# Packing the causal diagonal of a rational-softmax attention into equal pairs, on one NeuronCore

## The reference, cut to what matters

```
h     = x @ W[cat] + b[cat]
q,k,v = h @ w_qkv.T                       # 16 heads of 32
s     = (q . k) / sqrt(32) - slope * |i - j|,  NEG where j > i
num   = 0.5 * (1 + s * rsqrt(1 + s*s))
probs = num / (sum(num) + 1e-6)
x     = x + (probs @ v) @ w_out.T
z     = LayerNorm(x + relu(x @ W1 + b1) @ W2 + b2) * gamma + beta
x     = x + dequant(int8(z / scale) @ w_int8.T) + bias     # scale from max|z| of everything
```

## Time and profile before

| | us |
|---|---|
| Median of 3 runs | 2266.02 (2264.18 to 2266.58) |
| The profiled execution's own time | 2265.64 |
| Its span, first to last instruction | 2263.8 |
| Busy in the span: DVE | 1878.6 (83%) |
| PE | 1803.9 (80%) |
| POOL | 1715.7 (76%) |
| ACT | 1685.0 (74%) |
| Granted TensorE clock, mean | 0.907 of full speed |

### The profile page before, as it was taken

How to read it: one execution, slowest core, us unless ns; L and a number is a source line. 1 busy time by engine, 2 the same in 40 slices (tenths; PEclk the granted TensorE clock), 3 DMA queues, 4 the chain that set the end, 5 groups by cost and what they waited for, 6 DMA issues and landing times.

```text
span 2263.8 us, 31228 instructions
## 1 busy us (share of the span) xinstructions
PE 1803.9 (80%) x10640; PEld 904.5 (40%) x10640; DVE 1878.6 (83%) x2114; ACT 1685.0 (74%) x1938; POOL 1715.7 (76%) x784
## 2 busy tenths in 40 slices
PE   5678877877787789998888877877787787887864
PEld 4555323333333346664444433333333333342331
DVE  4358888888889888889789898888888888899768
ACT  0247897989889888889567667999889888767413
POOL 2136887788878887788678887788878887788548
PEclk9899988988898899999999998988988898998879
DMA  5411111110111022202322221110111021121137
GB/s 176 146 49 44 49 30 35 43 45 25 40 40 49 20 69 66 68 25 74 84 77 81 69 54 34 40 49 21 45 40 48 20 79 44 42 62 52 59 123 237
DMA packets 126620, 138.68 MB, mean 61 GB/s; under 512 B 27868, under 2 KB 78044, under 8 KB 126044
## 3 DMA queue, kind: packets, MB, share of 16 engines
q1 hardware_dynamic: 126460, 136.64, 21.5%
HBM read 54.02 MB, written 22.80 MB: 34 GB/s over the span
## 4 chain that ended last, share of the span: by engine, by line
PE 38%; ACT 21%; DVE 20%; issue 12%; POOL 4%; DMA 2%; SPq 2%; DVEq 0%; POOLq 0%; ACTq 0%
ACT yb L669 9%; PE sc L825 7%; PE ov L804 7%; ACT yb L671 7%; DVE gb L1042 6%; PE dn L804 6%; ACT gb L661 6%; DVE gb L983 5%; PE it L723 5%; PE it L740 4%; PE it L747 4%; PE it L727 3%; POOL oT L654 2%; SPq L428 2%; PE it L707 1%
## 5 line engine op out<-in xcount | busy, mean ns | idle before, releaser
L623 POOL TENSOR_TENSOR yb<-yb 128x1024 f32<-128x1024 f32 (+3 forms) x640 | 1510.2, 2373 | 460.9 <-DVE gb L1042 448.6
L669 ACT ACTIVATE yb<-sc 128x1024 f32<-128x1024 f32 (+3 forms) x640 | 566.9, 886 | 376.3 <-PE sc L825 189.8
L1042 DVE TENSOR_TENSOR gb<-sc,yb 128x1024 f32<-128x1024 f32 (+3 forms) x640 | 676.6, 1057 | 186.1 <-ACT yb L671 183.9
L983 DVE TENSOR_TENSOR gb<-gb,yb 128x1024 f32<-128x1024 f32 (+3 forms) x640 | 779.2, 1218 | 3.9 <-ACT gb L661 0.5
L825 PE MATMUL sc<-qmv,kst 128*128 128x512 f32 (+3 forms) x1280 | 505.6, 472 | 295.8 <-DVE gb L1042 278.2
L671 ACT ACTIVATE yb<-yb 128x1024 f32<-128x1024 f32 (+3 forms) x640 | 595.0, 930 | 20.3
L661 ACT ACTIVATE gb<-gb 128x1024 f32<-128x1024 f32 (+3 forms) x640 | 584.1, 913 | 0.1
L825 PEld LDWEIGHTS sc<-qmv,kst 128*128 128x128 f32 x1280 | 238.7, 209 | 648.3 <-DVE gb L1042 453.3
L804 PE MATMUL ov<-gb,vv 128*32 128x512 f32 (+3 forms) x2560 | 338.4, 604 | 18.0 <-DVE den L997 10.5
L804 PE MATMUL dn<-gb,ones 128*32 128x512 f32 (+3 forms) x2560 | 326.3, 584 | 0.0
L723 PE MATMUL it<-hT,wT 128*128 128x512 f32 x496 | 249.9, 629 | 5.8 <-DVE area L921 1.8
(11 more groups left out here) (112 smaller groups left out, 1093.5 us busy)
## 6 DMA issues: line engine op xcount, KB each, us to landing
qmv<-stage SPq DMA_DIRECT2D x384, 64.0 KB
kst<-stage SPq DMA_DIRECT2D x384, 64.0 KB
area<-in_x_dram SPq DMA_DIRECT2D x58, 256.0 KB, 2.8
out_dram<-oT SPq DMA_DIRECT2D x32, 256.0 KB, 3.3
den<-rec_d SPq DMA_DIRECT2D x31, 256.0 KB
wT<-wT_d SPq DMA_DIRECT2D x7, 768.0 KB, 4.4
x_d<-area SPq DMA_DIRECT2D x16, 256.0 KB, 2.6
z_d<-area SPq DMA_DIRECT2D x16, 256.0 KB, 3.2
```

Of the source, the lines that this page charges most:

```text
L623: pool.tensor_tensor(y, y, y, ALU.mult).then_inc(s_y2, 1)
L669: act.activation(y, sc[:, k % SLOTS, :, q0_of(g, k):], ACT.Square).then_inc(s_s2, 1)
L983: dve.tensor_tensor(t, t, yview(k)[:, :, q0:], ALU.add).then_inc(s_num, 1)
L1042: dve.tensor_tensor(gview(k)[:, :, q0:], sc[:, k % SLOTS, :, q0:], yview(k)[:, :, q0:], ALU.mult).then_inc(s_g, 1)
```

## The change

- **Equal pairs.** The diagonal is packed. Block 0 of the diagonal stays two pairs of 512 columns a head. Blocks 1 and 3 (384 and 128 columns) share a PSUM bank and make two pairs together. Block 2 (256 columns) takes four heads in one pair. A chunk's diagonal is five pairs of 1024 columns, where it was eight pairs of 1024 to 256; a group has 68 pairs in 36 units. Matmuls and masks are the same in number and width. ACT, DVE and POOL always take 1024 columns.
- **Waits.** PE waits for `k` and `v` of a chunk at the first diagonal pair or unit, no longer at the chunk's first.
- **Lags.** `LAG` = 6 counts pairs and means the same distance. `NORM_LAG` goes from 6 to 3, `NORM_LAG_LAST` from 2 to 1. DVE's steps stay one and three pairs behind SP's.
- **Items on ACT.** The emptying of `rt`, `a` and `zt` moves from DVE to ACT, behind ACT's three operations of the same pair, with a semaphore `s_evac_act` of its own. DVE keeps the maximum over |z| (`largest`), and does it after the next pair.
- **`norm` on POOL** gets one more small operation (`shift` = -mean*rstd).
- **Loops written out.** All eight groups are straight code, with waits on constants.
- Budget of a pair: the same as for a full pair before, everywhere.

Cut to its core:

```diff
-LAG = 3
-NORM_LAG = 6
-NORM_LAG_LAST = 2
+LAG = 6
+NORM_LAG = 3
+NORM_LAG_LAST = 1
...
+        def both(c, *blocks):
+            return [[Piece(2 * p + i, kb, q0, CH - q0, i, sum(CH - q for _, q in blocks[:n]))
+                     for i in range(2) for n, (kb, q0) in enumerate(blocks)] for p in range(HG // 2)]
+        for c in range(n_chunks):
...
+            for kb in range(TT * c):
+                unit(c, *both(c, (kb, 0)))
+            d = TT * c
+            unit(c, *both(c, (d, 0)))
+            unit(c, *both(c, (d + 1, P), (d + 3, 3 * P)))
+            unit(c, [Piece(h, d + 2, 2 * P, CH - 2 * P, h // 2, h % 2 * 2 * P) for h in range(HG)])
...
-            w = CH - self.width(k // 2)
-            left = max(-1.0, min(left, 0.5)) + (6 * w / 1200 + 0.5) - 1.35 * w / CH - 0.1 + slack
+            left = max(-1.0, min(left, 0.5)) + 6 * CH / 1200 - 0.95 + slack
...
-                p0 = 2 * (g.last[c] + LAG) + 1
+                p0 = g.last[c] + LAG
...
-    def for_groups(eng, body):
+    def for_groups(body):
         for b in range(B):
-            for hg0, g, count in runs(b):
-                if count == 1:
-                    body(b, hg0, b * NG + hg0, g, starts[b, hg0])
-                else:
-                    with eng.Fori(hg0, hg0 + count) as hg:
-                        body(b, hg, b * NG + hg, g, starts[b, hg0] - hg0 * len(g.items) + hg * len(g.items))
+            for hg, g in runs(b):
+                body(b, hg, b * NG + hg, g, starts[b, hg])
...
+                    pool.tensor_scalar(shift[:, a:a + 1], mv[:, a, 0:1], rstd[:, a:a + 1], -1.0,
+                                       ALU.mult, ALU.mult).then_inc(s_rstd[a], 1)
...
+                act.wait_ge(s_item, item + 1)
+                if what == "rt":
+                    if m:
+                        act.wait_ge(s_zst[a], 16 * m)
+                        act.wait_ge(s_amax, z_before)
+                    act.activation(resT[a], feat, ACT.Copy).then_inc(s_evac_act, 1)
+                elif what == "a":
+                    act.wait_ge(s_bw, 16 * 7 * (b + 1))
+                    act.activation(hid[a], bank[:, 0:P], ACT.Relu, bias=b1c[:, 0:1]).then_inc(s_evac_act, 1)
+                elif what == "zt":
+                    for k in range(KC):
+                        r = act.activation(resT[a][:, k, :], feat[:, k], ACT.Identity, scale=gam[:, k:k + 1],
+                                           bias=bet[:, k:k + 1])
+                    r.then_inc(s_evac_act, 1)
...
                 for k in range(PAIRS):
...
+                    act.activation(yview(n), sc[:, n % SLOTS], ACT.Square).then_inc(s_s2, 1)
+                    act.wait_ge(s_s2, n + 1)
+                    act.activation(yview(n), yview(n), ACT.Abs_reciprocal_sqrt, bias=1.0).then_inc(s_y, 1)
+                    if n >= NUM_LAG:
+                        one_plus_g_squared(n - NUM_LAG)
+                    for job in after_pair.get(k, []):
+                        d = b if g is ending else b - 1
+                        after(d, job, bases[0] + job.index, zs_before(d, job.name[1]))
...
+                        for what, at in (("q", g.first[c]), ("k", g.first[c] + 2 * TT * c)):
+                            if k == at:
+                                own = g.operands.index((what, c)) + 1 if (what, c) in g.operands else -(c == 0 and carry)
+                                pe.wait_ge(s_op, 16 * NPROJ * (ops_before(g, G) + own))
+                        for p in g.pairs[k]:
+                            out = slot[:, p.bank, p.at:p.at + p.width]
+                            diagonal = p.kb >= TT * c
```

More of the change, by code:

```diff
@@ L24 @@
 NORMED = 2
+ON_ACT = ("rt", "a", "zt")
 STAGED = 3
@@ L177, in adaln_attn_ffn @@
     plain = Group(NC, [], True)
-    first = [2 * u for u in plain.first] + [2 * len(plain.units)]
+    first = plain.first + [len(plain.pairs)]
     opening = Group(NC, [job for j in range(TT, KB)
```

393 lines of the change are left out of this document (223 added, 170 removed).

## The result

The median of four runs is 2233.8 us (2231.4 to 2238.5), against 2265.1 us for the kernel before on the same chip (four runs): ratio 0.9864, 95% interval 0.9851 to 0.9878. That is faster by 31 us, where 147 were forecast, and outside the range of 2070 to 2186.

A forecast was written before the change was run, and what follows sets the result against it. ACT bounds plain groups' full pairs, hand-overs their diagonals; PE bounds G3, DVE G4 and G7. Plain groups -79, G3 -8, G0 -13, G4 -21, G7 -26 sum to -147: from 2265.6 to 2119 us, range 2070 to 2186.

The forecast's parts named there:

- the whole group is 68 x 3.06 = 208.1: Plain groups: all 68 pairs would run at 3.06 us, the pace of full pairs in chunk 3, giving 208.1 us.
- A plain group: Each of G1, G2, G5, G6: 208.1 plus 2 for queries and 2.6 for stops, 212.7 us, so -19.8.
- G4: Group with after-attention work of 16 tiles: 1.10 times its busiest engine, PE at 269.3, giving 296 us, so -21.
- G0: Group with items like G3's, PE busy 226.4 of 280.1 us: between G3's gain and a plain group's, -13 us.
- G3: Group that makes the second sample's input: PE keeps 223.1 us of work, 3.5% idle gives 231 us, so -8.
- G7: Group with ten after-attention tiles: -9 us for chunks 0 and 1, -17 for chunks 2 and 3, together -26.
- Tail: Six tiles at the kernel's end: DVE's part shorter, POOL's chain longer; 0 us, bounds -3 and +3.
- PE keeps the diagonals long: Rival, chance 0.20: PE needs 17 us a diagonal instead of 15.3, ACT waits, +48 us; 2186 with G4 and G7 worse.
- ACT's own pace: Rival, chance 0.15: ACT runs at 2.89 us a pair without stops, -16 for each of four groups; say 2070 us.
- SP's queue: Rival, chance 0.05: SP's transfers late for every normalisation, DVE stops twice a chunk, 62 times; at 3 us each 2292 us.
- The packing gives nothing: Rival, chance 0.02: diagonals' time goes with matmuls, plain groups stay at 232, later ACT evacuations eat G4's gain; 2262 us.
- the tables' number: Rival, chance 0.03: ACT reloads its tables for Copy and Relu, two loads for each of 64 evacuations; 2209 us.

The follow-up runs named there:

- e12: Changed kernel with the next group's k of chunk 1 due before its v, and slack 1.2 instead of 0.8 in G4: 2211.3 us, ratio 0.9752.
- e3: Changed kernel with POOL's square over one bank of two: 2192.6 us.
- e17: Changed kernel with DVE's sum (the numerator) over one bank of two in every pair: 2178.8 us.
- e13: Changed kernel with all elementwise work of the diagonal pairs over one bank of two, in plain groups: 2189.2 us.
- e15: e12 with v of chunk 2 also projected in chunk 0, in groups that make no inputs: 2219.7 us, ratio 0.9807.
- e1: Changed kernel with rt, a and zt emptied by DVE again instead of ACT: 2248.7 us, ratio 0.9913.
- e2: Changed kernel with each division by the sum done over one column of 512: 2218.3 us.
- e5: Changed kernel with PE's products for the denominators done only for key block 0: 2209.4 us.

## Why the prediction was wrong, step by step

**The step that failed** is "the whole group is 68 x 3.06 = 208.1". The first half of it held: "the 85.3 us of diagonals become 20 pairs at the pace of full ones", 62.7 measured for 61.2. The second half took 3.06 us as a property of a full pair. It was an average over what else stood in chunk 3's full pairs at that time, 2.945 and stops; with the diagonals shortened, more of the products, a further division and evacuation and six longer sums fall in full pairs, and the average went to 162.4 / 48 = 3.38. ACT's idle time in G1 is nearly what it was (27.0 us before, 24.7 now): packing removed 5.1 us of its work and little waiting.

**Unpriced**: the due dates. The document ahead of the prediction says that their formulas stay, on shorter chunks; the sum has no term for it. The runs give 3.6 us a plain group for pair 60, and 22 us for e12 as a whole (25 by the ratios).

A plain group missed by 12.3 us. Of these the 3.6 for pair 60 are shown: the period of pair 60 was 2.95 us in all four groups before, and e12 takes its stop away. The 6 us for DVE's room and POOL's interference (e3, e17; the same 6, not twice) are what this costs in the changed kernel. The kernel before had it too, and no run halves the sum or the square there; what is new of it can only be estimated, from the 5.1 us by which the sums in full pairs got slower. The 2 us of e13 are a third part. That the three add up was not tested, and PE's slow-clock stops were not priced, so how the 12.3 us divide is open in the main.

**G4** failed with its factor, "I take 1.10: 296". ACT 238.3 and PE 275.7 came near the forecast (235 and 269.3), but the group is 1.20 times its busiest engine. The 1.118 from which the 1.10 was taken is the ratio to DVE, 316.9 / 283.4; to PE the group stood at 1.18 before, and that times 269.3 is 317, no gain at all. Slack alone gives 6 us back, e15 12, less PE work 9.5, half of DVE's sum 13.7. No single one brings 296, and what makes up the rest is open. That the evacuations on ACT stretch it, which the prediction expected, is refuted by e1. **G0** got no gain where 13 us were forecast. The burst that now stands on its pair 0 puts off its first multiplication by 37 us, but no run takes this burst or that of pair 6 away, so their price is not shown; e12 gives back 2.7 of the 4.6 us with both in place. **G3** stayed at 240.4 with PE busy 225.2: the forecast let PE's idle share fall to 3.5%, and it went from 6.8% to 6.3%. **G7** was right, 28.7 for 26, and e1 confirms ACT's part. **Tail**: +3.8 for 0, just past the +3 of the bound. The last division stands 6.5 us further behind the last multiplication than before, but the chain behind it has caught up by the last maximum over |z|, 54.2 us behind that multiplication where it was 54.3. So the loss lies in the int8 product behind it, and its cause is open.

**POOL's added operation** was priced with the wrong sign. It was to cost 0.6 us a tile, but it lets the large operation behind it multiply and add where that subtracted and multiplied, and the large one got cheaper by more. The first row is the kernel before, the others the one after:

```profile
L616 POOL TENSOR_SCALAR area<-area,mv,rstd 128x512 f32<-128x512 f32 x26 | 60.7, 2336 | 2.7
...
L665 POOL TENSOR_SCALAR area<-area,rstd,shift 128x512 f32<-128x512 f32 x26 | 33.8, 1300 | 2.6
...
L662 POOL TENSOR_SCALAR shift<-mv,rstd 128x1 f32<-128x1 f32 x32 | 12.9, 404 | 3.3
```

That is 1.70 us a tile where it was 2.34, and POOL's busy time in G4 went from 249.4 to 238.8 us where the prediction has 255.

**Small terms.** The queries for chunk 1 were priced at 2 us a group, with estimates of 2 us to land and 0.9 us for the scores; their transfers ran from 378.7 to 387.0, at once behind the group's start, since the item is now forced on pair 0, and no stop of pair 5 shows. ACT's stop at the group's start is 1.77 us, and it was 1.54 before, so the term should have been near nothing. The waits of DVE's inversion for its transfer, priced at 1.3 us each and 2.6 a group, are there, with the mechanism that was forecast but unequal, 0.46 and 3.20 us in G1, the second beyond the bound of 2.5:

```profile
DVE rec L1084 <- DMA rec<-den: 3.7, 2, 3.2
```

**The rivals.** "PE keeps the diagonals long" did not happen: they take 62.7 us. "ACT's own pace", 2.945 us a pair or 200.3 a group, was not reached. No table was loaded beside `Copy` or `Relu`; ACT's rows show two loads, at the first square and the first root, and none later, before and after. The Trainium skill, "ScalarE: Activation LUTs", section "Table sets: the hidden batching unit", says that such cheap functions are in every set, and the trace agrees. The 2.66 us that the prediction gives for a switch stand in another section of that page, "What ACT_TABLE_LOAD costs"; no switch fell between pairs here, so no run shows one. "SP's queue" made DVE stand for 3.7 us in G1, in two stops and not in two a chunk. "The packing gives nothing" lies 28 us from the time measured and the tables' number 25, nearer than any other, by luck: the diagonals did not go with their matmuls, they fell by 22.6 us, and ACT's evacuations did not eat G4's gain (e1).

## What to carry to other kernels

An average pace read from one stretch holds what else stood in that stretch; before multiplying it by a new count, split it into the undisturbed period and its stops, and ask where the stops' causes will stand afterwards. When a stage with room is shortened, list the work that lay in it and put it somewhere. If dates in a hand-made schedule count from a stage's ends, print the load of each slot before and after: here that costs nothing and shows the bursts of 6.88 at once. And a ratio of a stage to its busiest engine holds for that engine only.

## What the runs showed of the hardware

- A DVE operation on two SBUF inputs that begins inside one of POOL's squares waits for the square's end: a 128x1 multiplication took 1.84 us and ended within 0.01 us of it (e2). The 128x1024 sum takes 1.22 us when it begins first, and the square that begins 0.16 us behind it then takes 2.81 us, where the shortest of the run takes 1.89. In G1, 19 of 68 sums take 1.8 us: they begin some 2.1 us into a square and end 1.08 us behind its end; one begun 0.08 us into a square takes 2.89. The division of 128x512 takes 2.38 us in the same way (0.69 alone), while the multiplication that reads a score from PSUM takes 1.22 at all times. The Trainium skill, "SBUF — State Buffer", section "Who interferes with whom", says that such an instruction contends with a GpSimd instruction that reads SBUF, and that the shared pair of ports is an exclusive lock; the rows agree.
- Taking 28% of the matmuls from a PE with gaps lowered its granted clock from 0.92 to 0.79 and saved 3% of its busy time (e5, G1).
- On POOL a 128x512 operation with two per-partition operands took 2.08 us as subtract and multiply, and 0.77 as multiply and add (both in the tail), with 0.26 us for the 128x1 operation that this needs.
- On ACT a 128x512 Copy from PSUM took 585 ns, a 128x128 Relu with bias 351 and a 128x128 Identity with scale and bias 454, against 683, 338 and 400 on DVE: the sum of these six is 2.75 us a tile, and ACT's busy time in G4 is 37.9 us above that of G1, where the prediction's line over columns gave 1.95 a tile and 31.
